# Seven inner products for one of seven block products, with the next chunk's mixing moved

## The reference, cut to what matters

```
agg_w = einsum('bk,koi->boi', softmax(mlp(cond)), weight)     # a 64x64 mixing matrix for each of 64 samples
y     = einsum('boi,bih->boh', agg_w, x) + agg_b              # x is 64 x 64 x 1024
q(w)  = round(clip(w / (mean|w| + 1e-5), -1, 1))              # ternary weights
out   = x + ((y @ q(w_gate).T) * (y @ q(w_up).T)) @ q(w_down).T   # times the three mean|w|
```

## Time and profile before

| | |
|---|---|
| median of three runs | 1728.03 us |
| span of the profiled execution | 1726.1 us (first to last instruction) |
| time around the span, from the median | 1.9 us |
| TensorE busy | 1707.7 us, 99% of the span |
| VectorE busy | 1096.0 us, 63% |
| ScalarE busy | 575.6 us, 33% |
| GpSimd busy | 28.0 us, 2% |
| granted TensorE clock, mean | 0.999 of 2.4 GHz |

### The profile page before, as it was taken

One profiled execution on the slowest core, in us unless ns is written; L12 is line 12 of the kernel. 1 busy time (PEld: TensorE's weight loads), 2 busy tenths in 40 slices (PEclk: granted clock), 3 DMA queues, 4 the chain that ended last, 5 costly groups with the idle time before them and its releaser, 6 DMA issues.

```text
span 1726.1 us, 31355 instructions
## 1 busy us (share of the span) xinstructions
PE 1707.7 (99%) x12424; PEld 1215.6 (70%) x12424; DVE 1096.0 (63%) x1786; ACT 575.6 (33%) x921; POOL 28.0 (2%) x59
## 2 busy tenths in 40 slices
PE   6999999999999999999999999999999999999999
PEld 5554545968769596795958768596776959678684
DVE  6898895555766468554685646755576545855464
ACT  6887732312333133230333213231233313323120
POOL 0010000000000000000000000000000000000000
PEclk9999999999999999999999999999999999999999
DMA  8666626312242032420224211331223313132021
GB/s 342 249 229 239 221 96 219 121 44 97 76 148 96 22 108 77 168 66 22 107 102 164 65 75 54 129 137 43 97 76 126 101 40 108 65 124 79 29 87 49
DMA packets 59735, 194.06 MB, mean 112 GB/s; under 512 B 5280, under 2 KB 5600, under 8 KB 59584
## 3 DMA queue, kind: packets, MB, share of 16 engines
q1 hardware_dynamic: 56432, 177.49, 28.9%
q0 software_dynamic: 2560, 14.36, 2.2%
q10 hardware_dynamic: 592, 0.09, 0.0%
HBM read 160.90 MB, written 31.01 MB: 111 GB/s over the span
## 4 chain that ended last, share of the span: by engine, by line
PE 97%; DVE 2%; DMA 1%; issue 0%; ACT 0%; SPq 0%; DVEq 0%
PE ps L881 52%; PE ps L938 25%; PE ps L658 17%; PE ps L899 2%; PE ps L761 1%; DMA xa<-in_x_dram 1%; DVE wsum L1318 0%; DVE ys L1413 0%; DVE msk L1458 0%; DVE ys L1380 0%; DVE xa L1529 0%; DVE prod L1496 0%; DVE yp L1418 0%; ACT wdT L1106 0%; SPq L493 0%
## 5 line engine op out<-in xcount | busy, mean ns | idle before, releaser
L881 PE MATMUL ps<-yp,wgT 128*128 128x256 f16 x4116 | 902.4, 273 | 1.1 <-issue 1.1
L881 PE MATMUL ps<-wuT,wgT 128*128 128x256 f16 x4116 | 902.4, 273 | 0.0
L881 PEld LDWEIGHTS ps<-yp,wgT 128*128 128x128 fp8e4 x4116 | 402.9, 98 | 50.8 <-issue 2.9
L881 PEld LDWEIGHTS ps<-wuT,wgT 128*128 128x128 fp8e4 x4116 | 402.7, 98 | 48.3
L938 PE MATMUL ps<-wdT,inter 128*128 128x512 fp8e4 x1960 | 433.2, 379 | 0.0
L938 PEld LDWEIGHTS ps<-wdT,inter 128*128 128x128 f16 x1960 | 191.1, 98 | 227.2 <-issue 1.4
L1762 DVE SCALAR_TENSOR_TENSOR xr<-ps,osc,xr 128x512 f32<-128x512 f32 x210 | 156.4, 748 | 168.2 <-PE ps L938 128.4
L1711 DVE TENSOR_TENSOR wdT<-ps,msk 128x512 f32<-128x512 f32 (+1 forms) x77 | 51.3, 666 | 207.1 <-PE ps L881 207.1
L1241 ACT COPY raw<-ps 128x512 f32<-128x512 f32 (+1 forms) x77 | 43.7, 567 | 314.6 <-PE ps L881 314.0
L1248 ACT COPY msk<-ps 128x512 f32<-128x512 f32 (+1 forms) x77 | 43.6, 567 | 138.1 <-PE ps L881 138.1
L1263 ACT COPY inter<-ps 128x256 f32<-128x256 f32 x70 | 26.1, 372 | 180.1 <-PE ps L881 180.1
(11 more groups left out here) (229 smaller groups left out, 1497.9 us busy)
## 6 DMA issues: line engine op xcount, KB each, us to landing
wgT<-wcomb SPq DMA_DIRECT2D x70, 896.0 KB, 4.7
wdT<-dcomb SPq DMA_DIRECT2D x14, 2240.0 KB, 10.9
xa<-in_x_dram SPq DMA_DIRECT2D x8, 2048.0 KB, 7.8
out_dram<-xr SPq DMA_DIRECT2D x64, 256.0 KB, 2.0
wcomb<-xa POOLq DMA_DIRECT2D x17, 448.0 KB, 3.0
xr<-in_L_ffn_w_down_dram SPq DMA_DIRECT2D x9, 512.0 KB, 5.5
inter<-in_L_ffn_w_gate_dram SPq DMA_DIRECT2D x7, 512.0 KB, 16.6
wdT<-in_L_ffn_w_up_dram SPq DMA_DIRECT2D x7, 512.0 KB, 4.4
```

The lines of the kernel that those rows point to most:

```text
L881: last = nc.tensor.matmul(out, w, operand(i, OPERAND[what])[:, k, :], start=(start and h + k + i == 0), stop=(k == KQ - 1 and i == 1), ski ...
```

## The change

P2 of pairs 0 to 9 of chunks `c=2` to `c=7` is no longer 16 matmuls of 256 columns. The same fast scheme is used again inside it: the product's two weight halves, two halves of its inputs and two halves of its columns give seven inner products of 4 matmuls each, with 128 columns. ScalarE and VectorE carry partial results between them. `inner_a` does two of the seven, `inner_b` one, `inner_g` one and `inner_d` three. The four combined weight blocks of each pair are made by GpSimd in chunk `c=1` from the ring, written to DRAM (`wsub`) and loaded for each pair into one of two places. VectorE makes the four sums of the moving operand for each chunk (`inner_sums`), and both engines split them into parts.

The next chunk's mixing has two slices in each of pairs 2 to 5, its norms come in the first down group, and its `scales` and `scale_y` between the outputs of that group. The mixing matrices of all chunks are written to DRAM (`aggd`), and `next_x` loads the next chunk's into `ablk` ahead of x. Some waits of VectorE and SyncE are renumbered for the new order, and the second down weights are loaded at pair 10 in place of pair 8.

```diff
@@ SyncE
             def next_x(c):
                 sp.wait_ge(s_xr, NT * c)
                 sp.wait_ge(s_y, KH * c + KH)
+                for h in range(2):
+                    sp.dma_start(ablk[h * C:(h + 1) * C, :, h * C:(h + 1) * C],
+                                 aggd[h * C:(h + 1) * C, bass.ds((c + 1) * NT, NT), :]).then_inc(s_abd, 16)
                 load_x(c + 1)
...
@@ GpSimd, in chunk c=1
+            for p in range(NPR):
+                pool.wait_ge(s_ring[p % RING], 16 * (p // RING + 1))
...
+                    nc.gpsimd.tensor_tensor(st[:, 0], uk[0], gk[0], ALU.subtract, saturate=False).then_inc(s_subt, 1)
...
+                    nc.gpsimd.dma_start(wsub[p, q], sub_stage[q][p % 2]).then_inc(s_subw[p % 2], 16)
@@ TensorE
+            def inner(what, p, out, x, w, start=False):
+                for k in range(2):
+                    for i in range(2):
+                        wk = (blocks_s(sub_ring[INNER.index(what)][p % 2])[:, w, k, :] if isinstance(w, int)
+                              else ring(p, w[0], BLOCK[what], 2 * w[1] + k))
+                        last = nc.tensor.matmul(out, wk, inner_x(what, i, x)[:, k, :], start=(start and k + i == 0),
                                                stop=(k + i == 2), skip_group_check=True)
+            def inner_a(c, p):
...
+                    inner(what, p, lowers[:, q, 0], IA11, (0, 0), q == 0)
+                    last = inner(what, p, lowers[:, q, 1], IS1, 0)
+            def inner_b(c, p):
+                pe.wait_ge(s_e1, NPR * (c - FIRST - 1) + p + 1)
...
+            def inner_g(c, p):
+                pe.wait_ge(s_e2, NPR * (c - FIRST - 1) + p + 1)
...
+            def inner_d(c, p):
+                pe.wait_ge(s_ir, NPR * (c - FIRST - 1) + p + 1)
...
+                    inner(what, p, bank[:, 0:TH], IA12, (0, 1))
+                    inner(what, p, bank[:, 2 * TH:3 * TH], IS4, (1, 1))
+                    inner(what, p, bank[:, TH:2 * TH], IA22, 3).then_inc(s_done[what], 1)
@@ TensorE, pairs
+                    mix = [2 * (p - 2) + i for i in range(2) if more and p - 2 in range(KH // 2)]
                     product(c, p, "P1")
+                    if inners(c, p):
+                        plain5 = "P5" not in inners(c, p)
+                        inner_a(c, p)
+                        if p:
+                            product(c, p - 1, "P4")
+                        else:
+                            product(c, p, "P5", 0)
+                        inner_b(c, p)
+                        for k in mix[0:1]:
+                            conv(c + 1, k)
+                        product(c, p, "P6", 0)
+                        inner_g(c, p)
+                        product(c, p, "P6", 1)
+                        if plain5:
+                            product(c, p, "P5", None if p else 1)
+                        for k in mix[1:2]:
+                            conv(c + 1, k)
+                        if p:
+                            product(c, p - 1, "P3")
+                        inner_d(c, p)
+                        product(c, p, "P7")
+                        continue
@@ ScalarE, pairs
                     copy_p1(c, p)
-                    if p < 2:
+                    if inners(c, p):
+                        inner1(c, p)
+                    elif p < 2:
                         residual(c, 2 * p)
                         residual(c, 2 * p + 1)
                     if p:
                         gate21(c, p - 1)
+                    if inners(c, p):
+                        inner2(c, p)
+                        inner3(c, p)
                     copy_p16(c, p)
+                    if inners(c, p) and p < 2:
+                        residual(c, 2 * p)
+                        residual(c, 2 * p + 1)
@@ VectorE, pairs: c11 and i11 go behind sum4, inner_upper ahead of c12
-                    if p < NPR:
+                    if p < NPR and not inners(c, p):
                         c11(c, p)
                         i11(c, p)
...
+                    if inners(c, p):
+                        inner_upper(c, p)
...
+                    if inners(c, p):
+                        c11(c, p)
+                        i11(c, p)
```

More of the change, by code:

```diff
@@ L604, in _ @@
                 chunk(c)
+            sub_third(NC - 1)
             pairs(NC - 1)
@@ L831, in down, with product @@
                 last.then_inc(s_dn, 1)
-            def product(c, p, what):
+            def product(c, p, what, half=None):
                 n = NS * (c - FIRST) + p
@@ L872, in product @@
                     pe.wait_ge(s_c22, n + 1)
-                if p == 0:
+                if p == 0 and half != 1:
                     pe.wait_ge(s_ylo, KH * c + OPERAND[what] + 1)
-                waited(c)
-                for h in range(2 if p < NPR else 1):
+                if half != 1:
+                    waited(c)
+                for h in range(2 if p < NPR else 1) if half is None else (half,):
                     out = bank[:, h * HALF:(h + 1) * HALF]
@@ new lines, in inner_a @@
+            def inner_a(c, p):
+                n, done = NS * (c - FIRST) + p, DN * FIRST + ND2 * (c - FIRST)
+                half, later = NPR // 2, c - FIRST - 1
+                if p % 2 or NI == 1:
+                    pe.wait_ge(s_sub[p % 2], 16 * NI * (half * later + p // 2 + 1))
+                else:
+                    pe.wait_ge(s_sub[0], 16 * ((NI * half - 1) * later + NI * (p // 2) + 1))
+                if p == 0:
+                    pe.wait_ge(s_o, done)
+                    pe.wait_ge(s_ylo, KH * c + OPERAND[INNER[0]] + 1)
+                    pe.wait_ge(s_ilo, NI * later + 1)
+                elif p == GRP + 1:
+                    pe.wait_ge(s_o, done + len(DOWN[0]))
+                else:
+                    pe.wait_ge(s_c11, n)
+                    if NI == 2 and p == 1:
+                        pe.wait_ge(s_ilo, NI * later + 2)
+                    elif NI == 2:
+                        pe.wait_ge(s_c12, n - 1)
+                waited(c)
+                for q, what in enumerate(inners(c, p)):
+                    inner(what, p, lowers[:, q, 0], IA11, (0, 0), q == 0)
+                    last = inner(what, p, lowers[:, q, 1], IS1, 0)
+                last.then_inc(s_ia, 1)
@@ L943, in down_group @@
                     last.then_inc(s_dn, 1)
+                    if more and not g and d == 1:
+                        norms(c + 1)
                     if more and g and d == 4:
@@ L998, in pairs @@
                         product(c, p - 1, "P4")
-                    if more and p - 2 in range(KH):
-                        conv(c + 1, p - 2)
+                    for k in mix[0:1]:
+                        conv(c + 1, k)
                     product(c, p, "P6")
                     product(c, p, "P5")
+                    for k in mix[1:2]:
+                        conv(c + 1, k)
                     if p:
@@ L1816, in pairs @@
                     if p == GRP + 1:
+                        if more:
+                            add_l1(c + 1, KH - 1)
                         for d in range(len(DOWN[0])):
                             output2(c, 0, d)
-                    if p < NPR:
+                            if more and d == 2:
+                                scales(c + 1)
+                            if more and d - 3 in range(KH):
+                                scale_y(c + 1, d - 3)
+                    if p < NPR and not inners(c, p):
                         c11(c, p)
```

215 lines of the change are left out of this document (184 added, 31 removed).

## The result

The changed kernel takes 1744.67 us (median of 4 runs, 1741.84 to 1745.33) against 1728.12 us before (4 runs on the same chip). The ratio is 1.0094, 95% interval 1.0082 to 1.0106: slower by 0.9%, where 1726.6 us and 1716 to 1733 were predicted. The profiled execution took 1741.84 us with a span of 1740.0 us, against 1726.1 us of span before. One run of the kernel before that stands beside the last three experiments took 1983.59 us at a mean clock of 0.85, and their ratios leave it out.

The account below looks back on a forecast made before the run. The prediction took TensorE to bound the kernel (busy 99%, 97% of the chain). From a 1726.1 us span, less 11.4 saved, plus 10.0 stall, it got 1724.7, and 1726.6 us as median; range 1716 to 1733 (8 in 10).

Parts of the forecast that it names:

- TensorE's own work: P2 on TensorE: 28 matmuls at 55.6 ns take 1.557 us instead of 1.747, saving 0.190 a pair, 11.4 us.
- The load of x comes later: At each chunk's first mixing slice, x lands after it is wanted: TensorE stalls 2.0 us, five times, 10.0 us.
- The bounds, 1.5 to 2.8 us: Lower and upper end of TensorE's stall for x per chunk; 7.5 to 14 us in all.
- The forecast's own range: Total time of 1722.5 to 1731 us, given by the stall's bounds; the forecast's chance was 0.55.
- The chain inside P2: Four TensorE waits per pair behind copies, costed at nothing; up to 0.2 us in 36 tight pairs, 7 us.
- VectorE's new order, GpSimd and DMA: VectorE's reordered work in the down groups, GpSimd's subtractions in c=1 and the added loads: all costed at nothing.
- x in time: Rival: x arrives before the mixing slice and nothing is left of the stall; 1716.6 us, chance 0.20.
- The chain late: Rival: slow copies hold inner_g in the 36 tight pairs; 7 us more, 1733.6 us, chance 0.15.
- the loads' pace: Rival: weight loads hold 128-column matmuls to 81 ns each, 31 us more; 1769 us, chance 0.05.

Follow-up runs that it names:

- the last three experiments: before_x_late_1, before_x_late_2 and two_products; the kernel before, run beside them, took 1728.71 us (8 runs).
- early_copies: The changed kernel with the last two of ScalarE's four residual copies placed sooner, so x is asked for earlier: 1718.27 us, ratio 0.9947.
- filled_wait: The changed kernel with 26 more matmuls of 256 columns, of no use, ahead of TensorE's wait for x: 1734.36 us, ratio 1.0037.
- before_x_late_2: The kernel before, without inner products, its load of x held back until P7 of pair 1 is done: 1762.21 us, ratio 1.0197.
- x_ahead_of_ablk: The changed kernel with the load of x issued ahead of the two small loads into ablk: 1741.29 us, ratio 1.0073.
- before_x_late_1: The kernel before, without inner products, its load of x held back until P3 of pair 0 is done: 1738.51 us, ratio 1.007.
- two_products: early_copies with P5 by seven inner products too, in 9 of 10 pairs of each chunk: 1710.36 us, ratio 0.9898 to the kernel before.
- no_inner_products: The changed kernel with P2 kept as 16 matmuls and the old order of copies, all else of the change kept: 1728.51 us, ratio 1.0002.

## Why the prediction was wrong

The mechanism was named and stood where it was said; the size of one term was off, in two parts, and the larger part is a cost that the prediction put at nothing.

**TensorE's own work**: right. 0.190 us a pair, 55.6 ns a matmul, c=7 from its start to TensorE's end 195.62 us against 197.46, 1.84 shorter (1.9 predicted). The rule of the Trainium skill, "TensorE: Matmul & The Clock Gate", section Back-to-back issue gap (about 81 ns), does not hold here: the longest run of pairs, 24, goes at 55.8 ns.

**The load of x comes later**: this is the step that failed. It made 2.0 us a chunk and 10.0 in all; by the rows it was 4.45 a chunk (2.56 idle, 1.89 behind it) and 22.2 in all, which agrees with the 21.6 us that early_copies gives back between c=2 and c=7.

The first part is the delay. The copies ended where they should, but the two issues ahead took 0.86 and 0.79 us instead of 0.61 each, and x landed in 8.15 us instead of 7.7, together 0.9 us too little. Counted as the prediction counts, from the place where the slice would have begun, the slice was 2.6 to 2.84 us late (0.16 more than the idle times), 2.72 on average. The bounds, 1.5 to 2.8 us, held the average, and with it alone the time would have been 1730.2, inside the range.

The second part is what was left out: the clock behind each idle time, 1.63 us a chunk and 8.1 in all. I priced a stall at its own length and gave it an upper end by the same rule; the rows that were read had 1.00 in the clock's column throughout, since the kernel before had no idle time in its loop to show another value. filled_wait takes this part away alone, and before_x_late_2 makes it alone.

The Trainium skill, "DMA: Bandwidth & Descriptors", section Specifications (runs under 512 bytes are read, changed and written back), put the stall nearer its upper end. It ended there, but no run shows that this is the reason: x landed in 9.2 us with the small loads right behind it (x_ahead_of_ablk), and in 7.8 to 9.0 us in before_x_late_1 and before_x_late_2, which have no such load.

The forecast's own range, 1722.5 to 1731 "by the stall's bounds", was not quite theirs either: 7.5 to 14 us of stall give 1724.1 to 1730.6.

**The chain inside P2**: rightly costed at nothing; no wait stands at L983, in 60 pairs or with both products in two_products. ScalarE's copies of 128 columns took 0.27 us, as taken from the earlier trace rows.

**VectorE's new order, GpSimd and DMA**: right. One wait of 0.2 us for VectorE in the whole loop, and no_inner_products is level with the kernel before. GpSimd's subtractions took 0.65 to 0.87 us each, more than the copy of the earlier trace rows, and nothing waited for them.

**The rivals**: x in time gave 1716.6 us, and early_copies, where it is in time, took 1718.27; about 1.1 us of what is between is its 20 slices behind inner products, at 0.05 us each. The chain late would have given 1733.6 and the loads' pace 1769; neither came.

**What stays open.** The first pair began 2.3 us late in the profiled run. The clock stood at 0.50 to 0.60 there from 36 to 42 us, in the start-up, where the kernel before has 1.00. It is low there in x_ahead_of_ablk and two_products too, whose first pairs begin 1.9 and 1.0 us late, and at 1.00 in the five other kernels, whose first pairs are late by 0.3 us at most. Some of these have all of the change: nothing ties it to the change. Then the medians: early_copies and the changed kernel differ by 26.4 us, their profiled executions by 23.6, of which 2.05 are that late start and 21.6 the five chunks. What the runs without a profile lose beyond this can't be read.

## What to carry to other kernels

A wait put into a TensorE stream that has none is to be priced twice: its delay, and as a second term what the clock may take behind it, here 1.6 us behind every idle time of 2.35 us and more, and nothing behind six of 0.89 to 2.22. When a change reorders an engine off the critical path, follow its work up to the load whose buffer it frees, and place that first. If a short wait can't be avoided, compare it with filling it.

## What the runs showed of the hardware

- Behind idle times of 2.44 to 2.68 us (changed kernel) and 2.79 to 4.13 us (before_x_late_2) TensorE ran a while at half clock, for 1.6 to 1.7 us of loss each, one of them 2.4; behind six of 0.89 to 2.22 us (before_x_late_1) it did not. In x_ahead_of_ablk it did behind 2.35 to 2.72 us, and one of 2.05 us was enough too (its slice took 1.47 us, where it takes 1.15 behind a wait at full clock). So length alone did not decide near 2 us.
- The fall mostly began between the last moments of the idle time and a microsecond after it, and then cost the same. In the one case where the clock was down 1.46 us before the end (before_x_late_2, 1377.00) it cost most.
- A slice of mixing (8 matmuls of 128 columns) took 0.89 us behind a plain product, 0.95 right behind an inner product, and 1.15 behind a wait, all at full clock.
- Two small loads of 64 KB in runs of 256 bytes took 1.65 us of SyncE's queue ahead of x (518.03 to 519.68) and landed 2.4 to 2.5 us after their issue; behind x they landed after 7.5 and 8.2. x itself, 2 MB, landed after 8.15 us with them ahead of it, 9.2 with them behind it, and 7.8 to 9.0 in before_x_late_1 and before_x_late_2, which have none.
